# Third and fourth attention: each projection of a quad in two pieces of 256 columns, the copies from PSUM behind the second piece

## The reference, cut to what matters

```
x = x + tanh(g_xattn[2]) * L2_xattn(layernorm(x), ctx, ctx)   # 16 heads of 8 features
x = x + tanh(g_ffn[2])   * L2_ffn(layernorm(x))               # router: one of 8 experts per token
x = x + tanh(g_xattn[3]) * L3_xattn(layernorm(x), ctx, mask)  # causal within a sequence of 256, masked rows

q = layernorm(x) @ WQ ;  k = ctx @ WK ;  v = ctx @ WV         # 128 x 128 weights
out = softmax(q k^T / sqrt(8), over keys) @ v @ WO            # per head
```

## Time and profile before

| | us |
|---|---|
| runs: median (lowest to highest) of 3 | 1117.06 (1116.2 to 1119.53) |
| profiled execution: span from the first to the last instruction | 1124.8 |
| profiled execution: time outside the span | not given by the page |
| mean granted TensorE clock in the span | 0.907 |
| busy: PE, DVE, ACT, POOL | 932.1, 754.2, 677.1, 454.1 |
| third attention, first scores to last exponential | about 474 to 679 in the span |
| fourth attention | about 844 to 1053 |

### The profile page before, as it was taken

The page is one execution under the profiler, slowest core; times in us unless marked ns, Lnnn a source line. Parts: engine busy times, 40 slices in busy tenths (PEclk is TensorE's granted clock), DMA queues, the critical chain, the costliest instruction groups (busy, mean ns, idle before and its releaser), DMA issues.

```text
span 1124.8 us, 29016 instructions
## 1 busy us (share of the span) xinstructions
PE 932.1 (83%) x9406; PEld 555.3 (49%) x9416; DVE 754.2 (67%) x2004; ACT 677.1 (60%) x1462; POOL 454.1 (40%) x975
## 2 busy tenths in 40 slices
PE   3898889885758565799999886599958999999899
PEld 3644444443436333344545443277733555454698
DVE  3566777756978799778887772355584666667444
ACT  3556666646856566767776641155535777775466
POOL 5411112241134434301244344344458988877300
PEclk9999999995559777899999995599989999999999
DMA  6977656429999300000000000112131111111011
GB/s 186 155 88 82 47 45 47 38 29 238 179 181 174 97 1 1 1 1 2 2 15 15 14 11 19 39 51 60 54 84 58 40 58 40 59 55 43 6 36 35
DMA packets 285283, 67.07 MB, mean 60 GB/s; under 512 B 206241, under 2 KB 277985, under 8 KB 285154
## 3 DMA queue, kind: packets, MB, share of 16 engines
q1 hardware_dynamic: 279394, 50.94, 29.6%
q0 software_dynamic: 4896, 14.18, 3.7%
q10 hardware_dynamic: 864, 0.27, 0.1%
HBM read 34.80 MB, written 30.56 MB: 58 GB/s over the span
## 4 chain that ended last, share of the span: by engine, by line
PE 57%; DVE 21%; issue 8%; POOL 6%; ACT 3%; DMA 2%; SPq 2%; another core or an unknown queue 1%; DVEq 0%; ACTq 0%; POOLq 0%
PE bank L1132 14%; DVE nmax L1580 8%; PE bank L1164 6%; PE bank L1446 3%; PE bank L1431 3%; PE bank L1248 3%; PE bank L1146 3%; PE bank L1486 3%; PE bank L1478 2%; DVE stats L1515 2%; DVE small L1760 2%; PE bank L1257 2%; PE bank L1135 2%; PE bank L1122 2%; PE bank L1439 2%
## 5 line engine op out<-in xcount | busy, mean ns | idle before, releaser
L1580 DVE TENSOR_REDUCE nmax<-bank 128x8 f32<-128x1024 f32 x192 | 234.8, 1223 | 129.1 <-PE bank L1135 126.4
L823 ACT ACTIVATE probs_space<-bank 128x1024 f32<-128x1024 f32 x192 | 196.7, 1024 | 153.5 <-PE bank L1146 152.6
L1132 PE MATMUL bank<-q_one,k_all 32*128 32x512 f32 x768 | 221.5, 646 | 30.3 <-DVE nmax L1580 27.4
L1135 PE MATMUL bank<-k_one,q_all 32*128 32x512 f32 x768 | 218.4, 643 | 2.4 <-DVE nmax L1580 1.1
L1164 PEld LDWEIGHTS bank<-probs_space,vals 128*32 128x32 f32 x3072 | 74.3, 110 | 125.7 <-issue 124.1
L1164 PE MATMUL bank<-probs_space,vals 128*32 128x128 f32 x3072 | 127.8, 284 | 0.0
L1132 PEld LDWEIGHTS bank<-q_one,k_all 32*128 32x128 f32 x768 | 62.6, 187 | 59.9 <-issue 57.9
L833 ACT ACTIVATE k_one<-k_all,one_head 128x512 f32<-128x512 f32 x96 | 68.8, 722 | 20.8 <-DVE k_all L1606 19.3
L1146 PE MATMUL bank<-nmax_one,ones_bf 12*128 12x512 bf16 x384 | 79.3, 385 | 0.0
L576 POOL TENSOR_TENSOR var_b<-stats 128x8 f32<-128x8 f32 (+3 forms) x32 | 7.2, 225 | 178.4 <-DVE stats L1515 176.2
L649 POOL CAST nmax_parts<-nmax 128x16 bf16<-128x16 f32 x64 | 12.7, 199 | 162.9 <-DVE nmax L1580 121.4
(11 more groups left out here) (282 smaller groups left out, 2248.7 us busy)
## 6 DMA issues: line engine op xcount, KB each, us to landing
expert_rows<-zeros SPq DMA_DIRECT2D x8, 2128.5 KB, 31.8
late<-in_L_ffn_up_weights_dram POOLq DMA_DIRECT2D x9, 512.0 KB, 4.1
late<-_L_ffn_down_weights_dram POOLq DMA_DIRECT2D x9, 512.0 KB, 4.2
q_one<-expert_rows SPq DMA_DIRECT2D x40, 64.5 KB
q_scratch<-late SPq DMA_DIRECT2D x8, 256.0 KB
v_scratch<-moe_w SPq DMA_DIRECT2D x8, 256.0 KB, 3.4
vals<-v_scratch SPq DMA_DIRECT2D x8, 256.0 KB, 6.9
o_scratch<-o_tok SPq DMA_DIRECT2D x32, 64.0 KB, 3.1
```

What stands on the lines that cost most here:

```text
L823: act.activation(probs[:, 2 * g:2 * g + 2, :, :].rearrange("k g i q -> k (g i q)"), bank_pair[1][:, :, :].rearrange("k g f -> k (g f)"), A ...
L1132: pe.matmul(bank[2 + s], group(k_all, u, 2 * g + s), group(q_one, u, 2 * g + s), start=not masked, stop=False)
L1135: m = pe.matmul(bank[s], group(q_all, v, 2 * f + s), group(k_one, v, 2 * f + s), start=not masked, stop=True)
L1580: dve.tensor_reduce(nmax[:, u % 2, 0, :].rearrange("q (g i) -> q g i", i=HG)[:, 2 * g:2 * g + 2, :], bank_pair[0][:, :, :].rearrange("q g ...
```

## The change

For the third and fourth attention every projection is cut into two pieces, and the pieces of one projection stand in two half steps that follow each other: queries at the end of the second half of t = 4c-6 and in the first half of 4c-5; keys at the end of the second half of 4c-5 and in the first half of 4c-4; values (two matmuls of 128 columns each) at the end of the second half of 4c-4 and in the first half of 4c-3. ACT copies queries and keys no longer first thing in the iteration but between its two exponentials, behind the copy of the transposed rows, and the first one-head copy of the keys moves there with the key copy. The copy of the values stays where it is. Where a fill of three matmuls followed a projection of the fourth attention's first quad, one of two follows each piece. The first attention is left as it was.

On ACT:

```diff
+                def queries(c):
+                    past(act, "t_s1", 2 * (tiles + QT * (c - 1)))
+                    act.wait_ge(S("t_qp" if own else "t_xt"), (own_quads if own else 0) + c + 1)
+                    act.activation(q_all[:, c % 2, :], quad_bank(c), ACT.Copy, scale=SCORE_SCALE
+                                   ).then_inc(S("t_qa"), 1)
...
                 def iteration(t):
-                    c = quad(t, 5)
-                    if c is not None:
-                        past(act, "t_s1", 2 * (tiles + QT * (c - 1)))
-                        act.wait_ge(S("t_qp" if own else "t_xt"), (own_quads if own else 0) + c + 1)
-                        act.activation(q_all[:, c % 2, :], quad_bank(c), ACT.Copy, scale=SCORE_SCALE
-                                       ).then_inc(S("t_qa"), 1)
-                    c = quad(t, 4)
-                    if own and c is not None:
-                        past(act, "t_s2", 2 * (tiles + QT * (c - 1)))
-                        act.wait_ge(S("t_kp"), quads + c + 1)
-                        act.activation(k_all[:, c % 2, :], quad_bank(c), ACT.Copy).then_inc(S("t_kn"), 1)
+                    if not own and quad(t, 5) is not None:
+                        queries(quad(t, 5))
...
-                    if quad(t, 4) is not None and (own or t > -3):
+                    if not own and quad(t, 4) is not None and t > -3:
                         one_head_keys(quad(t, 4), 0)
...
                         act.activation(xnT_quad[:, :], quad_bank(c), ACT.Copy).then_inc(S("t_xe"), 1)
+                    if own and quad(t, 5) is not None:
+                        queries(quad(t, 5))
+                    c = quad(t, 4)
+                    if own and c is not None:
+                        past(act, "t_s2", 2 * (tiles + QT * (c - 1)))
+                        act.wait_ge(S("t_kp"), quads + c + 1)
+                        act.activation(k_all[:, c % 2, :], quad_bank(c), ACT.Copy).then_inc(S("t_kn"), 1)
+                        one_head_keys(c, 0)
```

On PE, the new functions:

```diff
+                HALF = QT * P // 2
+
+                def query_half(c, half):
+                    at = slice(half * HALF, (half + 1) * HALF)
+                    if half == 0:
+                        pe.wait_ge(S("t_xe"), own_quads + c + 1)
+                    m = pe.matmul(quad_bank(c)[:, at], wq, xnT_quad[:, at], start=True, stop=True)
+                    if half == 1:
+                        m.then_inc(S("t_qp"), 1)
+                    if masked and c == 0:
+                        fill_wait(2, 3)
+
+                def key_half(c, half):
+                    at = slice(half * HALF, (half + 1) * HALF)
+                    if half == 0:
+                        pe.wait_ge(S("t_qa"), quads + c + 1)
+                    first = QT * P * c + half * HALF
+                    m = pe.matmul(quad_bank(c)[:, at], wk, contextT[:, first:first + HALF], start=True, stop=True)
+                    if half == 1:
+                        m.then_inc(S("t_kp"), 1)
+                    if masked and c == 0:
+                        fill_wait(2, 3)
+
+                def value_half(c, half):
+                    if half == 0:
+                        pe.wait_ge(S("t_kn"), quads + c + 1)
+                    for j in range(2 * half, 2 * half + 2):
+                        m = pe.matmul(quad_bank(c)[:, j * P:(j + 1) * P], tile_of(contextT, QT * c + j), wv,
+                                      start=True, stop=True)
+                    if half == 1:
+                        m.then_inc(S("t_vp"), 1)
+                        if c == 0:
+                            fill_wait(8, 3)
```

In the first half of an iteration, before `pair_of_scores(t, 1, t + 2, 0)`:

```diff
+                    if own and c is not None:
+                        query_half(c, 1)
...
+                    if own and quad(t, 4) is not None:
+                        key_half(quad(t, 4), 1)
+                    if own and quad(t, 3) is not None:
+                        value_half(quad(t, 3), 1)
```

At the end of the second half, in place of the whole projections:

```diff
+                    if own and quad(t, 6) is not None:
+                        query_half(quad(t, 6), 0)
+                    if own and quad(t, 5) is not None:
+                        key_half(quad(t, 5), 0)
+                    if own and quad(t, 4) is not None:
+                        value_half(quad(t, 4), 0)
```

More of the change, by code:

```diff
@@ L1225, in iteration @@
                     c = quad(t, 5)
-                    if c is not None and (own or c > 0):
+                    if own and c is not None:
+                        query_half(c, 1)
+                    elif c is not None and c > 0:
                         pe.wait_ge(S("t_qa"), quads + c + 1)
-                        if own:
-                            pe.matmul(quad_bank(c), wk, contextT[:, QT * P * c:QT * P * (c + 1)],
-                                      start=True, stop=True).then_inc(S("t_kp"), 1)
-                            if masked and c == 0:
-                                fill_wait(3, 3)
-                        else:
-                            pe.wait_ge(S("a_ctxT"), c + 1)
-                            for j in range(QT):
-                                m = pe.matmul(bank[5][:, j * P:(j + 1) * P], tile_of(contextT, QT * c + j), wk,
-                                              start=True, stop=True)
-                            m.then_inc(S("t_kp"), 1)
+                        pe.wait_ge(S("a_ctxT"), c + 1)
+                        for j in range(QT):
+                            m = pe.matmul(bank[5][:, j * P:(j + 1) * P], tile_of(contextT, QT * c + j), wk,
+                                          start=True, stop=True)
+                        m.then_inc(S("t_kp"), 1)
+                    if own and quad(t, 4) is not None:
+                        key_half(quad(t, 4), 1)
+                    if own and quad(t, 3) is not None:
+                        value_half(quad(t, 3), 1)
                     pair_of_scores(t, 1, t + 2, 0)
@@ L1271, in iteration @@
                         m.then_inc(S("R_rank"), 1)
-                    c = quad(t, 6)
-                    if own and c is not None:
-                        pe.wait_ge(S("t_xe"), own_quads + c + 1)
-                        pe.matmul(quad_bank(c), wq, xnT_quad[:, :], start=True, stop=True).then_inc(S("t_qp"), 1)
-                        if masked and c == 0:
-                            fill_wait(3, 3)
-                    c = quad(t, 3)
-                    if own and c is not None:
-                        pe.wait_ge(S("t_kn"), quads + c + 1)
-                        for j in range(QT):
-                            m = pe.matmul(quad_bank(c)[:, j * P:(j + 1) * P], tile_of(contextT, QT * c + j), wv,
-                                          start=True, stop=True)
-                        m.then_inc(S("t_vp"), 1)
-                        if c == 0:
-                            fill_wait(8, 3)
+                    if own and quad(t, 6) is not None:
[4 more added lines that the diff above has]
+                        value_half(quad(t, 4), 0)
                     if not own:
```

## The result

| | kernel before | changed kernel |
|---|---|---|
| runs beside each other, median (lowest to highest) | 1118.23 (1112.21 to 1120.01), 7 | 1126.37 (1123.34 to 1128.62), 7 |
| ratio, 95% interval | | 1.0069 (1.0039 to 1.0099) |
| profiled execution: time, span | span 1124.8 | 1127.77, span 1126.0 |
| start of the third attention | 20.4 | 24.7 |
| third attention, exponential (0,0) to (31,1) | 197.3 | 189.4 |

Forecast were 1119.1 and a range up to 1124.0. The medians say +8.1, the two profiles +1.2. The profile shown of before has stalls in the third attention that this profile has not, though the changed kernel's half steps are longer elsewhere.

What follows compares the result with a forecast made beforehand. The prediction took the attentions as a loop of PE scores, ACT exponential and DVE maximum, without slack at the exponential. Third attention +3.0 and fourth -1.0 gave +2.0 on the median 1117.06: 1119.1, range 1113.5 to 1124.0.

Steps and rivals of the forecast that it cites:

- (8,0): Fourth attention, half step from tile 8's first exponential: key copies lengthen ACT's chain, 3.69 against 2.82, +0.87.
- (7,0): Fourth attention, half step from tile 7's first exponential: query copy between the exponentials, 3.51 against 3.27, +0.2.
- the values' saving: Fourth attention, second half of tile 9: the value projection leaves, 3.57 becomes 2.80, -0.77.
- L952 later by 1.4: Third attention's start: ACT's last feed-forward copy L952 comes 1.4 late, behind the query copy and a norm.
- Quad 7 of the fourth attention: No norms left on ACT, -0.39 in both long chains, and its query projection showed more: -0.95.
- start, full clock: Third attention's start: first scores wait for later query and key copies, +2.8, bounds +1.4 and +3.2.
- quads 2 and 3: Third attention, no routing on PE yet: queries, keys and values save, key copy costs; -0.5 each, -0.9 both.
- quads 4 to 7: Third attention with scatters: savings end in the wait, late exponential of t = 4c-4 costs +0.2 each, +0.8 for four.
- The 0.87 is swallowed and the quad gains 0.7: Fourth attention, quad 5: dear step falls on tile 16, 4.12 long because POOL is late; quad gains 0.7.
- The dear step: Half step with second key piece, key copy and one-head copies in ACT's chain: +0.87 in the fourth attention.
- the rival of 0.2: Full clock lost in the start or after scatters of quads 4 to 6: +3 to +6, 1122 to 1125; chance 0.2.
- The rival on the fast side: The gains stand: ACT's chain in (8,0) and (7,0) shorter, or part given back; about 1113, to 1107; chance 0.2.

Runs made afterwards that it cites:

- rebalanced: Changed kernel with first quads whole and five one-head copies a fourth-attention quad moved to the top of the next iteration; 1127.30, ratio 1.0028 to the kernel before.
- after_later: Changed kernel with four small POOL memsets ahead of each quad's four scatters; ratio 1.0163 to the kernel before.
- after_plain: Changed kernel with router rows written by plain DMAs in token order instead of scatters, experts' rows thereby wrong; 1116.76, ratio 0.9911 to the kernel before.
- before_plain: Kernel before with router rows written by plain DMAs in token order instead of scatters, experts' rows thereby wrong; 1111.46, ratio 0.9863 to the kernel before.
- before_norms: Kernel before with the last layer's first eight tiles' norms moved from POOL's tile 16 to behind its last butterfly step; ratio 0.9969.
- before_later: Kernel before with four small POOL memsets ahead of each quad's four scatters; ratio 1.0031 to the kernel before.
- start_whole: Changed kernel with only the third attention's first quad as before, whole projections and old copy places; ratio 1.0088 to the kernel before.
- after_again: The changed kernel unedited, run and profiled again beside the other follow-ups; ratio 1.0116 to the kernel before.
- before_again: The kernel before unedited, profiled once more; 1126.24, one run.
- fourth_only: Pieces and moved copies in the fourth attention only, third as in the kernel before; ratio 1.0020 to the kernel before.
- fourth_moved: Third attention as before; fourth in pieces except its first quad, late one-head copies moved to the next iteration's top, POOL's norms moved; 1119.56, ratio 0.9936.
- values_only: Kernel before with only the values of quads 1 to 7 in two pieces, queries, keys and their copies unchanged; 1127.93, ratio 1.0026.

## Why the prediction was wrong

**Right, by its steps.** ACT's chains: (8,0) 3.75 for 3.69, (7,0) 3.54 for 3.51, and in the third attention 3.76 for 3.69 and 2.93 for 2.89; the values' saving (3.57 to 2.80); the length of a piece; L952 later by 1.4. rebalanced shows the chain to be the cause. The start came out at 22.9 in the one kernel with pieces that had the full clock all through it (after_later, granted 1.00), against 20.4: +2.5 for +2.8. Quad 7 of the fourth attention gained 0.65 to 0.8 for 0.95. Four routed quads without stalls cost 0.9 together (after_plain less before_plain, t = 10 to 25), for 0.8.

**Wrong.** The measured +8.1 against +2.0 leaves 6.1 to explain. Taken from the profiles, stage by stage, for executions without stalls ("plain pair" is after_plain less before_plain):

| term | forecast | measured | from |
|---|---|---|---|
| start, full clock | +2.8 | +2.5 | after_later |
| third attention, quad 1 | +0.3 | +0.5 | plain pair |
| quads 2 and 3 | -0.9 | -0.3 | plain pair |
| quads 4 to 7 | +0.8 | +0.9 | plain pair |
| fourth attention | -1.0 | +0.9 | plain pair |
| clock in the start | 0 | +1.8 | changed kernel, 24.7 less 22.9 |
| clock in tiles 26 and 27 | 0 | +2.4 | plain pair, 14.6 less 12.2 |

The measured terms add up to 8.7, an estimate from several profiles, near the 8.1. The steps that failed are therefore the fourth attention, forecast as a gain, and the clock, put at nothing in the sum; quads 2 and 3 add 0.6. The clock's share in the seven executions is not shown, only in the profiled ones.

*The fourth attention: "The 0.87 is swallowed and the quad gains 0.7"* (quad 5). It lost 0.5. The dear step did not run beside POOL's lateness but began behind it, since PE's key piece stands behind the transpose that waits for POOL (961.71 above). In addition POOL bounds the stretch up to there: in the kernel before it waited for DVE for 2.5 in all, so gains of more than that ahead of tile 16 could not count, and losses could. Quads 3, 4 and 6 cost 0.3 to 0.5 each for 0.17. The whole was +0.1 in the two profiles shown and +0.9 in the plain pair, for -1.0.

*The clock.* This was the rival of 0.2. after_plain and the changed kernel's profile lose 2.2 in (27,1), before_plain nothing, with 1.00 granted there:

```profile
648.00:653.00 5.00, 3.86 (x44) 2.05 (x44) 4.51 (x13) 1.47 (x2) 0.00 (x0) 1.00 0.00 0
653.00:658.00 5.00, 4.60 (x61) 2.66 (x61) 4.12 (x13) 2.66 (x5) 1.64 (x8) 1.00 0.00 0
```

In the window before the fall the changed kernel's PE is busy 3.23 of 5. That the slow clock is the default and activity releases it (the Trainium skill, TensorE: Matmul & The Clock Gate, Part 1) agrees with that row in direction only: in (27,0) before_plain's PE is busy 2.35 of 4.33 and keeps 1.00. Nor is the loss the change's alone. Of seven profiles with the third attention as before, three lose the clock near there (the one shown, before_norms, before_later); of the seven with the changed kernel's steps there all but start_whole do. The start is alike: of the five profiles with pieces in it the granted clock falls in four, which take 23.4 to 25.5, and in five of the eleven with the old start it was low too, and they take 22.0 to 22.3 instead of 20.4. That the change makes the clock fall more often is likely by this count and not shown.

*Quads 2 and 3 of the third attention*, -0.9 forecast, gave -0.3. The forecast had no routing on PE yet, but the transposes of the router's rows begin in (7,0) and its matmuls in (7,1): (7,0) is 3.03 for 2.89 and (7,1) 2.88 for 2.62. (6,1), still without them, is 2.84 for 2.66.

*The stalls: "What queries and values save there ends in that wait", "+0.2 each".* The forecast let the stalls stay as they were. Where the changed kernel has stalls, in after_again, this step failed by more than any other: quads 4 to 7 take 108.9 there and 100.2 in before_again (and in before_norms, fourth_only and fourth_moved), +8.7 for +0.8, of which 0.9 is there without stalls. Most of the 13.4 beside after_again is this. In the comparison above that gave +8.1 the stalls probably had no share. The profiled execution had none and the other six are as short. Of the kernel before the seven executions took 1112.2 to 1120.0; before_again less its 8.6 of stalls would be 1117.7, an estimate, beside their median of 1118.2. Why quads 5 to 7 pay 3 to 4 each instead of 0.7 is open. In the kernel before PE multiplied the values, 1.0 of work, in the half step that is stalled anyway ((13,1) is 3.61 without the stall and 4.67 with it), and the change emptied that half step and filled others; but values_only, which does only that, takes 1.6 more in these three quads and not 8.

*The side.* The rival on the fast side fell: nothing of ACT's cost came back. By the medians of the plain pair the change costs 5.3 without stalls, inside the range; the 8.1 measured first lies outside it.

## What to carry to other kernels

Splitting work to fit gaps helps only if what waits for the last piece also has a gap: here the copies landed between two exponentials, and moving them once more, to where ACT idles, gave the quad its 1.0. Before counting a gain, ask whether a third engine with hardly any idle time runs the stage; take its load off first. And where a half step is stalled from outside, work that stands in it can be nearly free: values_only moved the values out of it, and quads 5 to 7 did not get shorter (76.4 for 74.8).

## What was unexpected of the hardware

Around four DMA_INDIRECT of 0.96 to 1.26 on POOL, ACT and DVE stood for 0.2 to 3.5 with no releaser named, and with plain DMAs never. One execution of the changed kernel had none of this, another of the same program had 15 us of it, with the scatters at the same place (0.27 and 0.11 after the exponentials) and POOL's four instructions equally long. By their times (1123.3 to 1128.6, and 1137.0 to 1144.0) the other executions beside each were like it in this, an estimate. The Trainium skill (SBUF — State Buffer, SBUF: two separate sides) tells of DVE holding up POOL's descriptors; POOL's durations show nothing of that here, and by that section ACT never waits on the port that DVE and POOL share. What holds the engines was not found.
